# A state scan's steps in three fp32r passes instead of one fp32 matmul

## The reference

```python
h = relu(depthwise_conv(fake_quant(emb)[x], taps=2))          # (8, 512, 128)
h = h + attn(layernorm(h))                                    # a linear state scan
h = h + ffn(layernorm(h))                                     # 8 experts, two GELU layers
```

```python
state[t] = state[t-1] @ A + u[t] @ B        # from init_states; u is the normalised h
x[t] = exp(2) * state[t] / max|state[t]|    # over the whole of each head
y = x @ C + u @ D
```

## Time and profile before

| | us |
|---|---|
| median of 3 runs (171.99 to 172.4) | 172.16 |
| time of the profiled execution | 172.16 |
| its span, first to last instruction | 170.4 |
| PE busy | 160.6 (94%) |
| DVE, ACT, POOL busy | 130.5, 101.0, 101.5 |
| first state step starts | 48.98 |
| last copy of the first group's states starts | 57.66 |

### The profile page before, as it was taken

The page is one execution under the profiler, slowest core; times in us unless marked ns, Lnnn a source line. Parts: engine busy times, 40 slices in busy tenths (PEclk is TensorE's granted clock), DMA queues, the critical chain, the costliest instruction groups (busy, mean ns, idle before and its releaser), DMA issues.

```text
span 170.4 us, 3456 instructions
## 1 busy us (share of the span) xinstructions
PE 160.6 (94%) x1149; PEld 137.8 (81%) x1149; DVE 130.5 (77%) x403; ACT 101.0 (59%) x236; POOL 101.5 (60%) x168
## 2 busy tenths in 40 slices
PE   5987989998999999999999989999999999989992
PEld 1676875896666789987679889999999999989991
DVE  3979959735548375897995998989989898649893
ACT  3048999362124532323436857958779587788991
POOL 4437777659997035361223594896978969785000
PEclk9999999999999999999999999999999999999999
DMA  5995000000000000000000000010010100110022
GB/s 138 391 427 254 6 0 2 0 6 0 0 0 0 4 0 0 0 6 0 0 0 0 0 4 0 0 67 0 0 67 0 63 0 4 62 62 2 4 104 83
DMA packets 2182, 7.47 MB, mean 44 GB/s; under 512 B 238, under 2 KB 748, under 8 KB 1908
## 3 DMA queue, kind: packets, MB, share of 16 engines
q1 hardware_dynamic: 2146, 7.23, 11.1%
q10 hardware_dynamic: 18, 0.02, 0.1%
HBM read 5.15 MB, written 2.10 MB: 43 GB/s over the span
## 4 chain that ended last, share of the span: by engine, by line
PE 79%; POOL 6%; ACT 5%; DVE 4%; issue 3%; DMA 2%; ACTq 0%; POOLq 0%
PE bank L1308 12%; PE bank L1288 12%; PE bank L1237 8%; PE bank L1152 6%; PE bank L1146 5%; PE bank L1083 4%; PE bank L1234 4%; PE bank L1033 4%; PE bank L1257 4%; PE bank L1089 4%; PE bank L1114 2%; PE bank L1264 2%; POOL rstd L517 2%; PE bank L1058 2%; PE bank L1006 2%
## 5 line engine op out<-in xcount | busy, mean ns | idle before, releaser
L534 POOL TENSOR_TENSOR hid_p<-hid_f,hid_p 128x256 fp32r<-128x256 f32 x48 | 34.1, 735 | 13.8 <-ACT hid_p L684 13.8
L682 ACT ACTIVATE hid_f<-bank,pa 128x256 f32<-128x256 f32 x64 | 30.8, 491 | 15.9 <-PE bank L1288 14.2
L1288 PE MATMUL bank<-xaT_p,fc_p 128*128 128x256 f32 x192 | 35.0, 293 | 0.2 <-issue 0.2
L1308 PE MATMUL bank<-hid_p,out_hi 128*128 128x256 f32 x128 | 32.5, 290 | 1.0 <-POOL hid_p L534 1.0
L1288 PEld LDWEIGHTS bank<-xaT_p,fc_p 128*128 128x128 f32 x192 | 26.7, 189 | 0.4 <-issue 0.3
L1308 PEld LDWEIGHTS bank<-hid_p,out_hi 128*128 128x128 f32 x128 | 23.4, 188 | 2.0 <-POOL hid_p L534 1.4
L684 ACT ACTIVATE hid_p<-bank,pa 128x256 fp32r<-128x256 f32 x48 | 23.4, 487 | 0.0
L1237 PE MATMUL bank<-pb,xh 128*128 128x128 f32 x128 | 19.5, 275 | 0.0
L517 POOL TENSOR_TENSOR rstd<-spread,neg_half 128x8 f32<-128x8 f32 x8 | 13.6, 1697 | 9.5 <-DVE spread L943 9.5
L1308 PE MATMUL bank<-hid_p,out_lo 128*128 128x256 f32 x64 | 17.8, 278 | 0.0
L1237 PEld LDWEIGHTS bank<-pb,xh 128*128 128x128 f32 x128 | 16.9, 192 | 0.0
(11 more groups left out here) (156 smaller groups left out, 373.6 us busy)
## 6 DMA issues: line engine op xcount, KB each, us to landing
fc_w<-in_fc SPq DMA_DIRECT2D x2, 2048.0 KB, 11.4
out<-res SPq DMA_DIRECT2D x7, 256.0 KB, 2.0
pa<-in_pack_a SPq DMA_DIRECT2D x1, 407.0 KB, 3.2
pb<-in_pack_b SPq DMA_DIRECT2D x1, 384.0 KB, 4.8
out<-res SPq DMA_DIRECT2D x2, 128.0 KB, 1.7
pw<-in_pack_a SPq DMA_DIRECT2D x1, 64.0 KB, 3.3
emb_w<-in_emb SPq DMA_DIRECT2D x1, 62.5 KB
conv_w<-in_conv ACTq DMA_DIRECT2D x1, 1.0 KB
```

Source lines behind the costliest of these rows:

```text
L534: nc.gpsimd.tensor_tensor(hid_p[1][:, half, c, :], hid_f[:, m % HID_SLOTS, :], hid_p[0][:, half, c, :].bitcast(F32), ALU.subtract).then_in ...
L682: full = nc.scalar.activation(hid_f[:, m % HID_SLOTS, :], src, ACT.Gelu, bias=bias)
L1288: last = mm(fc1_bank(8 * b + n)[:, 0:HALF], fc1_p[w][:, e * HID + c * P:e * HID + (c + 1) * P], xaT_p[m][:, b % 2, half, :], start=(k == 0 ...
L1308: last = mm(out_bank(b, half)[:, half * HALF:(half + 1) * HALF], out_p[w][:, e, c * CH:(c + 1) * CH], hid_p[m][:, half, c, :], start=(c == ...
```

## The change

The first group's second and third state steps (`q` = 1 and 2, four matmuls) become three fp32r passes each. Parts of `A` are made once, parts of a state after each of the first two steps of each half. The parts lie in blocks of `out_lo` and `out_hi` that are filled later. New semaphores: `a_hi`, `a_lo`, `s_hi`, `s_lo`.

```diff
+        def state_split(a, part):
+            return out_p[1][:, NE - 2 * NP + 2 * a + part, :]
+
+        def a_split(part):
+            return out_p[0][:, NE - 1, part * P:(part + 1) * P]
...
                 def copy_state(g, n):
                     q, a = divmod(n, NP)
                     act.wait_ge(state_done[g], n + 1)
+                    if g == 0 and q < RUN - 2:
+                        nc.scalar.activation(state_split(a, 0), scan_bank(a), ACT.Copy).then_inc(s_hi, 1)
                     nc.scalar.activation(every_run(g, a, q + 1), scan_bank(a).rearrange("p (b r k) -> p b r k", b=GB, k=NCH),
                                          ACT.Copy).then_inc(x_ready[g], 1)
...
+                def split_a():
+                    nc.scalar.activation(a_split(0), a1, ACT.Copy).then_inc(a_hi, 1)
...
+                split_a()
                 copy_out_prep(N_PREP - 1)
                 copy_runs(1, 0)
...
-                for n in range(GB):
-                    split_low(1, n)
+                def state_low(n):
+
+                    q, a = divmod(n, NP)
+                    dve.wait_ge(s_hi, n + 1)
+                    dve.wait_ge(x_ready[0], n + 1)
+                    view = "p (b r k) -> p b r k"
+                    nc.vector.tensor_tensor(state_split(a, 1).rearrange(view, b=GB, k=NCH), every_run(0, a, q + 1),
+                                            state_split(a, 0).bitcast(F32).rearrange(view, b=GB, k=NCH),
+                                            ALU.subtract).then_inc(s_lo, 1)
+
+                dve.wait_ge(a_hi, 1)
+                nc.vector.tensor_tensor(a_split(1), a1, a_split(0).bitcast(F32), ALU.subtract).then_inc(a_lo, 1)
+                state_low(0)
+                state_low(1)
+                split_low(1, 0)
+                state_low(2)
+                split_low(1, 1)
+                state_low(3)
+                split_low(1, 2)
+                split_low(1, 3)
...
                     if q >= 1:
                         pe.wait_ge(x_ready[g], n - 1)
+                        if g == 0:
+                            pe.wait_ge(s_lo, n - 1)
...
-                    mm(scan_bank(a), a1, every_run(g, a, q), start=False, stop=True).then_inc(state_done[g], 1)
+                    if g == 0 and q >= 1:
+                        pe.wait_ge(a_lo, 1)
+                        for k, (w, m) in enumerate(PARTS):
+                            last = mm(scan_bank(a), a_split(w), state_split(a, m), start=False, stop=(k == len(PARTS) - 1))
+                    else:
+                        last = mm(scan_bank(a), a1, every_run(g, a, q), start=False, stop=True)
+                    last.then_inc(state_done[g], 1)
```

More of the change, by code:

```diff
@@ L224, in build @@
         ks_done, ks_ready = [sem(f"ks_done{g}") for g in range(NG)], [sem(f"ks_ready{g}") for g in range(NG)]
+        a_hi, a_lo, s_hi, s_lo = sem("a_hi"), sem("a_lo"), sem("s_hi"), sem("s_lo")
         full_ready = sem("full_ready")
```

## The result

The median went from 172.19 to 173.51 us (four runs each): the ratio is 1.0077, with a 95% interval of 1.0063 to 1.0092. The change costs 1.3 us, between 1.1 and 1.6. Of all runs of all kernels here one is left out of its ratio: a single run of e4 took 315.43 us, where its four others took 171.41 to 171.73.

What follows compares the result with a forecast made beforehand. The prediction took TensorE (PE) as the bound, busy 94% of the span. Two stalls of 1.26 and 0.82 us less 0.62 saved gave +1.46: 172.16 + 1.46 = 173.6 us, range 172.8 to 174.6.

Steps and rivals of the forecast that it cites:

- Saving 0.62 us on PE: Four state steps on PE: three fp32r passes replace two fp32 passes, saving 4 x 0.155 us if nothing waits.
- A's parts hidden: A's high part (0.28 us) fits ACT's idle 1.06 us; its low part (0.28) on DVE is done before the first state.
- rival C: Port turns go worse: A's low part takes 1.09 us and the copies do not overlap, giving 174.6 us; chance 10%.
- Stored state 1.13 us after the step's end: On ACT, the high part goes ahead of the stored state, ready 1.13 us after the step's end instead of 0.64.
- Low part 0.68, the first one longer in a turn with GpSimd: DVE's state subtraction takes 0.68 us undisturbed; the first, blocked by GpSimd's first cast, ends about 52.30.
- From low part to streaming 0.16 us: Hand-over from DVE's low part to PE's first streaming of the next input takes 0.16 us.
- No stall ahead of the fourth and sixth: PE is still busy when the low parts of states 1 and 3 are ready, so those inputs do not wait.
- Sum +1.46 us at the end of the states: Stalls of 1.26 and 0.82 us ahead of the third and fifth inputs, less 0.62 saved, delay the sixth step's end.
- All of it passed on: Every engine waits for the end of the states, so the whole 1.46 us reaches the kernel's time.
- Rival B: The stall exists but is absorbed later, where the chain passes to POOL and DVE; 172.2 us if full; chance 5%.
- Rival D: PE's clock falls to 1.2 GHz for the twelve passes behind the first stall, giving 176.4 us; chance 3%.
- rival A: Ahead of the third and fifth inputs, idle ACT and DVE hide the conversions, so the saving stays: 171.5 us; chance 4%.

Runs made afterwards that it cites:

- e4: Changed kernel, but the three-pass steps take parts of the group's input instead of state parts, without state conversions or their waits: 171.61 us, ratio 0.9963 to the kernel before.
- e2: Changed kernel with its conversions and waits, but the state step is the single fp32 matmul of before: 174.16 us, ratio 1.0108 to the kernel before.
- e8: The changed kernel timed and profiled again, nothing altered: ratio 1.0088 to the kernel before.
- e1: Changed kernel with PE's wait for the low part moved from ahead of the input to the state step: 172.4 us, ratio 1.0016 to the kernel before.

## Why the prediction was right

- *Saving 0.62 us on PE:* right; e4 shows 0.60. In the changed kernel it was 0.66: a round of input and step took 1.40 us (54.74 - 53.34, 58.45 - 57.05) where it was 1.565 before, and there are four.
- *A's parts hidden:* right. The high part took 0.30 in ACT's idle time, whose rest was still 0.85 us. The low part took 0.28, not the 1.09 of rival C.
- *Stored state 1.13 us after the step's end:* right, the copies start 0.49 apart (49.45 and 49.94) in each of the pairs.
- *Low part 0.68, the first one longer in a turn with GpSimd:* right. The first took 0.88, and I had allowed for 1.0 (51.30 to 52.30). Issued at 50.63 inside the cast 50.35 to 50.97, it ended 0.54 us after that, the figure of the earlier trace rows. The forecast should have used it: 51.64 + 0.54 = 52.18, not 52.30, and a sum of 1.34 us. The second was issued at 51.92, just ahead of the cast at 51.94; there the cast waited, and it took 0.69 where I had supposed a second turn. PE was busy then, so it made no difference.
- *From low part to streaming 0.16 us:* a little more, 0.23 (51.51 to 51.74). With the quicker first low part it gives 1.20 us for the first stall (1.26 predicted) and 0.91 for the second (0.82). The second link as a whole, from the step's end (52.45 + 0.86 = 53.31) to streaming (55.45), took 2.14 us, where I had 2.07.
- *No stall ahead of the fourth and sixth:* right.
- *Sum +1.46 us at the end of the states:* measured 1.20 + 0.91 - 0.66 = +1.45, and +1.45 between the copies. The mechanism was right, but the agreement to 0.01 us is luck: the first low part was put 0.13 us too late, two hand-overs 0.07 too short and the saving 0.04 too small, and these nearly cancel.
- *All of it passed on:* right, 112.7 and 112.9 us behind the last copy. Rival B falls.
- *Clock:* a granted 1.00 in the stretch with both stalls, the upper level. Windows of the trace after (stretch, length, busy time of PE, PEld, DVE, ACT, POOL, clock), against the earlier trace rows:

```profile
48.25:57.05 8.80, 7.17 (x26) 4.59 (x26) 6.21 (x10) 4.35 (x8) 5.71 (x7) 1.00 0.00 0
57.05:65.00 7.95, 7.95 (x47) 6.92 (x46) 5.54 (x11) 3.96 (x7) 1.69 (x2) 1.00 0.01 2
```

Rival D falls. DVE and ACT are still idle for 29% and 51% of the stretch; rival A, which took that for cover, falls because one state's conversion is serial, and e2 shows what waiting for it costs.

The time, 173.51 against a forecast of 173.6 us, fits as well; the measured difference (1.1 to 1.6 us) is less sharp than the distance in the profile.

## What to carry to other kernels

Cheaper matmul passes are worth their saving only if the operands' conversion fits in the other work of the engine between a result and its next use. Add up that link first (here 2.07 us by the forecast, 2.14 measured, against 1.25 us of cover), not the busy shares of the converting engines. When a link is too long, look at where the wait stands in the queue before giving up: the same conversions cost 1.45 us with the wait ahead of three independent passes, 0.17 with it behind them, and allowed the whole gain once the link was cut short (low part read from PSUM) and the inputs had banks of their own (the two were only tried together). When a collision on a shared resource is moved, look at what it meets next.

## What the runs showed that I had not expected

Of two colliding operations the one issued first goes first, even by 0.02 us. The first low part (issued inside a cast) took 0.88 us. The second, issued at 51.92, took 0.69, and the cast behind it 1.15 instead of 0.61:

```profile
51.94 1.15 POOL L504 CAST hid_p<-uT 128x512 fp32r<-128x512 f32 x1
```

In e8 and e1 the subtraction was 0.03 us ahead of the cast (53.17 and 53.20, 52.48 and 52.51), with the same outcome. And the start of the kernel moves by over a microsecond between profiles (the first state copy at 49.45 and 50.69 in two profiles of the same kernel, of which the ids' cast, 4.18 and 4.81, has 0.63 and the sixteen matmuls behind it 0.43), nearly as much as the whole change. A distance inside the profile was the same to 0.01 us in both.
